# A decoder layer with a mixture of experts on one core: new order in the attention rounds, and the first shared unit made inside their last ones

## The chip, the cores and the metric

The kernel runs on 1 core of one Trainium2 chip. The metric is the device time of one execution in microseconds (us). Before the change it is 1107.71 us, the median of 3 runs (1106.47 to 1108.61).

## The reference, cut to what matters

Three blocks, each followed by a layer norm, on `x` of shape (32, 128, 256) in float32:

```
x = layernorm(x + attention_1(x))        # einsum('nqhd,nkhd->nhqk') on a transposed Q, K: in each token its 16 heads attend to one another
x = layernorm(x + cross_attention(ctx, ctx, x))   # one head of width 256
x = layernorm(x + ffn(x))
def ffn(X):                                   # B x S = 4096 tokens of width 256
    h = rmsnorm(X, norm1_w); q, k, v = h @ wq, h @ wk, h @ wv      # 16 heads of 16
    X = X + softmax(q k^T / 4) v @ wo
    h2 = rmsnorm(X, norm2_w)
    topw, topi = top_k(softmax(h2 @ router_w), 2); topw = softmax(topw)
    shared = (silu(h2 @ sh_gate) * (h2 @ sh_up)) @ sh_down         # 256 -> 512 -> 256
    spec   = sum over the two chosen of 8 experts of topw * (silu(h2 @ e_gate) * (h2 @ e_up)) @ e_down
    return X + shared + spec
```

## The kernel before, in words

All products are made to nearly full float32 precision from two float32r parts: a value is split into `hi` (a copy on ScalarE, ACT) and `lo` (value minus hi, on VectorE, DVE, or GpSimd, POOL), and each product is hi x hi + hi x lo + lo x hi, three matmuls.

**Phase A** (`phase_a`) is the attention part: 16 pairs of batch rows, 256 tokens each. The work on a pair is cut into jobs. Names ending in 1 belong to the first attention (`qk1`, `s1`, `t1`, `o1`, `out1`), names with x to the cross attention (`qx`, `sx`, `pvx`, `vo`), names ending in 3 to the third (`q3`, `k3`, `v3`, 16 heads over 128 tokens, scores `s3`, transposed scores `s3t`, `pv3`, `out3`), and `turn_h2`, `logits`, `turn_lg` make the router's logits. `SCHEDULE` (lines 65 to 86) gives for each engine an ordered list of (job, lag). In iteration `it` an engine runs its list from front to back, each job on pair `it - lag` if that is between 0 and 15. So each engine has one fixed order, written out by hand, and what decides the time is where an engine has to wait for another. The same job can stand at the end of a list with lag L or at its front with lag L+1: the order is the same, only the seam of the list is elsewhere. I write `v1`(15) for job v1 of pair 15.

`BANK` (line 87) gives each TensorE job its PSUM bank. A job waits until the last reader of the bank's previous user is done (`bank_users`, `LAST_READ`); for `o1_0`, `o1_1` that reader is the DVE multiply `o1e_0`, `o1e_1` (line 821), for `s3_0` it is the maximum `max3_0` (line 875), for `pv3_1` the DVE job `e3_1`.

SP (`@block.sync`) issues the DMAs in its own list's order and waits in that order too. `load_q1`, `load_k1`, `load_v1` bring the first attention's operands back from scratch memory; `load_k1` and `load_v1` are eight DMAs each, of 32 KB, into the block diagonals `kbd` and `vbd` (line 338). `s1` needs the first two, `o1` needs `vbd`. `load_kept` (line 349) waits for `qk1_0`, `qk1_1` and `v1` of pair 15, since the shared weights take the room of the first attention's weights, and then issues three weight loads of 512 KB and two token loads of 256 KB. It stands ahead of iteration 19 (`PAIRS + 3`).

**Phase B** (`phase_b`) is the feed-forward part in units of 256 tokens: 8 shared units, then 40 expert tiles (31 full ones and 9 of half size) with gathered rows, then 8 shared units. A unit is, on TensorE, the gate and up products in two halves (`gate_up(n, 0)`, `gate_up(n, 1)`, 24 matmuls each) and the product down (`down_unit`, 24). `gate_up(n + 1, h)` waits until DVE's `product(n, h)` has read the PSUM banks. ACT makes silu (its own table load, as exp has), then `product_hi`; DVE makes `product`, `product_lo`, `tok_lo`. The routing runs on DVE between the halves of the first units, placed by `ROUTING` (line 1783): choose the two experts, count (with two matmuls of TensorE), find slots, spread them as 0/1 matrices (`hits`, `lefts`), which TensorE multiplies in `invert` in units 4 and 5; `read_inverse` then gives the row lists with which POOL gathers rows (`fetch_tile`). `place` gives the table of experts, for which SP waits before it loads the first expert's weights (`load_expert(0)`). POOL makes half of the spread matrices (line 1871) in two instructions.

At the seam between the phases all engines join. Before the change the first tokens and the shared weights are split there, and unit 0's products follow.

At the end POOL adds the experts' results to the sums by accumulating DMAs, one group of `TOTALS` after the other (line 1917), DVE takes moments (`finish`, by `FINISHED`), ACT normalizes (`normalize`, by `NORMALIZED`), SP stores.

## Time and profile before

| | |
|---|---|
| device time, median of 3 | 1107.71 us (1106.47 to 1108.61) |
| the profiled execution | 1107.43 us, its span 1105.6 us |
| mean granted TensorE clock | 0.976 |
| TensorE busy | 1006.2 us, 91% |
| DVE busy | 838.6 us, 76% |
| ACT busy | 675.1 us, 61% |
| POOL busy | 506.3 us, 46% |

The span runs from the first to the last instruction. Phase A ends near 594 us, the shared units run until about 689, the expert tiles until about 1010. Busy shares are means over stages. A row of the timeline has the start, the duration, engine, line, operation, output and inputs, the shape and the number of instructions merged; in brackets stands the idle time of the engine just before and what ended it. A row without a bracket followed the engine's previous instruction at once. "PEclk" is the granted TensorE clock as a share of full speed.

### The profile page before, as it was taken

What the parts mean: (1) busy time and instruction counts of PE and PEld (TensorE: products, weight loads), DVE (VectorE), ACT (ScalarE), POOL (GpSimd) and SP (SyncE); (2) the same over time, 40 slices, a digit from 0 to 9 for tenths busy, and PEclk for the clock granted to TensorE, in tenths of its full rate; (3) what the DMA queues carried; (4) which work ended last, traced back from release to release, by engine and by line L of the source; (5) the groups of instructions that cost most, each with busy time, mean ns of one, the idle gap of its engine ahead of it and who ended that gap; (6) DMA issues with size and microseconds to landing.
All of it is one profiled execution on the core that took longest, in us unless ns stands there. A gap on an engine that the chain in (4) does not pass through costs nothing. (4 is left out here: it accounts for less than half of the span.)

```text
span 1105.6 us, 30332 instructions
## 1 busy us (share of the span) xinstructions
PE 1006.2 (91%) x11710; PEld 939.2 (85%) x11710; DVE 838.6 (76%) x1564; ACT 675.1 (61%) x1435; POOL 506.3 (46%) x525
## 2 busy tenths in 40 slices
PE   5789999999999999998765889999999999999984
PEld 4678888888888888887654889999999999999984
DVE  2767888888888888887665895878888888886445
ACT  2246556667655667666654333777777777775335
POOL 4254454455454455445321022566766556563222
PEclk9999999999999999999986999999999999999998
DMA  7864354544554444441312314689887777761973
GB/s 204 159 104 85 58 106 77 109 101 84 107 107 87 100 104 81 94 88 40 106 36 86 73 34 154 226 247 359 261 277 264 239 271 240 272 239 53 209 172 114
DMA packets 273711, 161.22 MB, mean 146 GB/s; under 512 B 213473, under 2 KB 238945, under 8 KB 272929
## 3 DMA queue, kind: packets, MB, share of 16 engines
q1 hardware_dynamic: 262576, 127.62, 43.0%
q0 software_dynamic: 9408, 29.18, 10.0%
q10 hardware_dynamic: 1584, 2.49, 0.7%
q8 instruction: 94, 1.54, 0.6%
q14 instruction: 49, 0.39, 0.1%
HBM read 120.54 MB, written 38.70 MB: 144 GB/s over the span
## 5 line engine op out<-in xcount | busy, mean ns | idle before, releaser
L1884 POOL DMA_INDIRECT kept_weights<-h_scratch,source_row x71 | 99.1, 1396 | 122.2 <-DVE tok_lo L1733 84.5
L1893 POOL DMA_INDIRECT results_scratch<-kept_late,result_row x71 | 95.0, 1339 | 50.5 <-ACT kept_late L1449 33.3
L1431 ACT ACTIVATE act_hi<-prod 128x512 fp32r<-128x512 f32 x94 | 59.3, 631 | 75.9 <-DVE prod L1744 74.5
L687 ACT ACTIVATE p3t<-psum 128x512 f32<-128x512 f32 x128 | 68.7, 596 | 48.0 <-PE psum L533 48.0
L1744 DVE TENSOR_TENSOR prod<-kept_weights,up 128x512 f32<-128x512 f32 (+1 forms) x112 | 71.6, 640 | 26.1 <-PE up L1315 14.4
L1402 ACT ACTIVATE we_hi<-w_raw 128x1024 fp32r<-128x1024 f32 x81 | 85.7, 1058 | 5.4 <-PE down L1337 5.4
L961 POOL TENSOR_TENSOR ctx_lo<-ctx_t,ctx_hi 128x512 fp32r<-128x512 f32 x16 | 20.5, 1283 | 124.9 <-ACT ctx_hi L597 124.9
L875 DVE TENSOR_REDUCE max<-psum 128x16 f32<-128x2048 f32 x32 | 73.2, 2287 | 5.0 <-PE psum L519 4.7
L1424 ACT ACTIVATE kept_weights<-gate 128x512 f32<-128x512 f32 (+1 forms) x112 | 62.3, 556 | 24.0 <-PE gate L1315 22.8
L1753 DVE TENSOR_TENSOR act_lo<-prod,act_hi 128x512 fp32r<-128x512 f32 x94 | 65.7, 699 | 13.7 <-ACT act_hi L1431 13.4
L378 PE MATMUL psum<-kept_room,x_hi 128*128 128x512 f32 (+1 forms) x256 | 61.5, 363 | 11.9 <-POOL x_lo L957 11.9
L1720 DVE TENSOR_TENSOR we_lo_second<-w_raw,we_hi 128x1024 fp32r<-128x1024 f32 x42 | 51.3, 1221 | 12.0 <-issue 8.1
L378 PEld LDWEIGHTS psum<-kept_room,x_hi 128*128 128x128 f32 x256 | 41.7, 194 | 19.1 <-issue 14.9
L907 DVE RECIPROCAL rden<-rden 128x256 f32<-128x256 f32 x32 | 56.1, 1753 | 1.1
L1720 DVE TENSOR_TENSOR we_lo<-w_raw,we_hi 128x1024 fp32r<-128x1024 f32 x39 | 47.6, 1219 | 8.8 <-ACT we_hi L1402 8.1
L1315 PE MATMUL gate<-tok_hi,we_hi 128*128 128x256 f32 x248 | 51.3, 288 | 0.0
L1449 ACT ACTIVATE kept_late<-down,slot_weights 128x256 f32<-128x256 f32 x71 | 30.1, 470 | 33.1 <-PE down L1337 33.0
L1315 PE MATMUL up<-tok_hi,we_hi 128*128 128x256 f32 x248 | 50.0, 283 | 0.0
L1315 PE MATMUL up<-tok_lo,we_hi 128*128 128x256 f32 x248 | 50.0, 283 | 0.0
L1315 PE MATMUL gate<-tok_lo,we_hi 128*128 128x256 f32 x248 | 49.9, 283 | 0.0
L968 POOL TENSOR_TENSOR x_res<-x_res,b_o 128x512 f32<-128x512 f32 x16 | 21.0, 1313 | 62.2 <-DMA x_res<-in_x 62.2
L1337 PE MATMUL down<-we_hi,act_hi 128*128 128x256 f32 x284 | 48.0, 291 | 0.0
(335 smaller groups left out, 3455.7 us busy)
## 6 DMA issues: line engine op xcount, KB each, us to landing
w_raw<-in_w_gate SPq DMA_DIRECT2D x27, 512.0 KB
w_raw<-in_w_up SPq DMA_DIRECT2D x27, 512.0 KB
w_raw<-in_w_down SPq DMA_DIRECT2D x27, 512.0 KB
raw_gate<-in_w_gate SPq DMA_DIRECT2D x13, 512.0 KB
passed<-in_w_up SPq DMA_DIRECT2D x13, 512.0 KB
passed<-in_w_down SPq DMA_DIRECT2D x13, 512.0 KB
x_t<-in_x_t SPq DMA_DIRECT2D x16, 256.0 KB, 3.4
q_scratch<-qk SPq DMA_DIRECT2D x16, 256.0 KB, 2.4
```

Source lines behind the costliest of these rows:

```text
L378: mm = pe.matmul(dst, x(dk), y(dk), start=(n == 1), stop=(n == 3 * DK))
L687: act.activation(p3t[:, a, 4 * j:4 * j + 4, :], bank[f"s3t_{a}"][:, 512 * j:512 * (j + 1)].rearrange("p (h n) -> p h n", h=4), ACT.Exp)\
L875: half_step(dve.tensor_reduce(max3[:, a, :], bank[f"s3_{a}"].rearrange("p (h n) -> p h n", h=H), AX.X, ALU.max, negate=True))
L1315: mm = pe.matmul(bank[:, fi * UT:(fi + 1) * UT], wp[:, kind, dk * DFF + f * P:dk * DFF + (f + 1) * P], hp[:, n % 2, dk, :], start=(m == 0) ...
L1402: act.activation(w_hi[:, kind, :], raw_of(use)[kind], ACT.Copy).then_inc(w_hi_done, 1)
L1424: act.activation(used(silu[:, h, :], n), used(gate[h][:, :], n), ACT.Silu).then_inc(silu_done, 1)
L1431: act.activation(act_hi[:, n % 2, h * FH:(h + 1) * FH, :], prod[:, h, :].rearrange("p (f n) -> p f n", f=FH), ACT.Copy).then_inc(act_hi_do ...
L1720: dve.tensor_tensor(w_lo[:, kind, :], raw_of(use)[kind], w_hi[:, kind, :].bitcast(F32), ALU.subtract).then_inc(w_lo_done, 1)
L1744: dve.tensor_tensor(used(prod[:, h, :], n), used(silu[:, h, :], n), used(up[h][:, :], n), ALU.mult).then_inc(prod_done, 1)
L1753: dve.tensor_tensor(act_lo[:, n % 2, h * FH:(h + 1) * FH, :], prod[:, h, :].rearrange("p (f n) -> p f n", f=FH), act_hi[:, n % 2, h * FH:( ...
L1884: pool.indirect_dma_start(out=slot_rows[:, i % 2, j, :], out_offset=None, in_=by_token, in_offset=bass.IndirectOffsetOnAxis(ap=source_row[ ...
L1893: pool.indirect_dma_start(out=scratch["results"], out_offset=bass.IndirectOffsetOnAxis(ap=result_row[:, at:at + 1], axis=0), in_=y_rows[:, ...
```

## The change

1. `SCHEDULE` and `BANK` are replaced. Seen as one endless order, the differences are: on TensorE `to1_1` before `turn_h2`; `logits` before `s3t_0`; `s3t_0` before `qk1_0`; `s3t_1` before `qk1_1`; `s1_1`, `pv3_0`, `out3`, `turn_lg` in this order; `v1` behind `pv3_1`; `q3` before `t1_1`; `o1_0` before `vo`. On ACT `norm_h`, `exp1_0` and `h_hi` stand so that `pvc_0` follows `h_hi`; `sq_h2` and `norm_h2` stand behind `x_hi` and `qxe`; `lgc` behind `ctx_hi`. On DVE `den1_0` and `h_lo` stand before `e3_0`, `r3_0` follows `e3_0` at once, `o1e_0` stands before `voe`, `o3_lo` behind `qk1_1e`, `x3` behind `sub1_1`. On POOL `x_lo` is first after `norm_x1`, and `sum` follows `o3e_1`. On SP `load_ctx` goes before `load_res`, `store_h2` stands between `load_k1` and `load_q1`, `store_sum` before `load_v1`.
2. `load_kept` stands ahead of iteration 17 (`PAIRS + 1`). With the new seam of SP's list, iteration 17 begins with `store_sum`(9), `load_v1`(14), `store_q1`(15).
3. The shared weights' hi parts are made on ACT behind `x1_hi`(15), `qxe`(15), `expx`(15), their lo parts on DVE behind `x1_lo`(15), `voe`(15), `bn2`(15); two units' tokens behind `pxe`(15) on ACT and `h_lo`(15) on DVE.
4. Unit 0's gate and up halves are made on TensorE ahead of `turn_h2`(14) and `turn_h2`(15).
5. In phase B unit 0 has only silu, products and down left; the routing starts half a unit to a unit later; POOL's spread is cut into pieces of 4 picks; `TOTALS`, `FINISHED` and `NORMALIZED` are reordered.

```diff
@@ constants
-FINISHED = (0, 0, 0, 2, 4, 8, 10, 14)
-NORMALIZED = (0, 0, 0, 0, 2, 4, 8, 10)
+FINISHED = (0, 0, 0, 2, 4, 8, 12, 14)
+NORMALIZED = (0, 0, 0, 0, 2, 4, 8, 12)
...
+    "pe": [
+        ("t1_0", 2), ("turn_x1", 3), ("q3", 4), ("t1_1", 2), ("k3", 4), ("o1_0", 2), ("vo", 3), ("s3_0", 4),
+        ("qx", 3), ("o1_1", 2), ("to1_0", 2), ("sx", 3), ("tm_0", 4), ("s3_1", 4), ("to1_1", 2), ("turn_h2", 6),
+        ("turn_px", 3), ("v3", 4), ("pvx", 3), ("logits", 6), ("s3t_0", 4), ("qk1_0", 0), ("tm_1", 4), ("out1", 2),
+        ("s3t_1", 4), ("qk1_1", 0), ("s1_0", 1), ("s1_1", 1), ("pv3_0", 4), ("out3", 5), ("turn_lg", 6),
+        ("turn_h", 3), ("pv3_1", 4), ("v1", 0),],
...
+        ("max3_0", 5), ("o1e_1", 3), ("o1lo_0", 3), ("maxx", 4), ("qs_0", 5), ("max3_1", 5), ("recx", 4),
+        ("o1lo_1", 3), ("z2", 4), ("bn2", 4), ("qs_1", 5), ("qk1_0e", 1), ("y1", 3), ("bn1", 3), ("qk1_1e", 1),
+        ("o3_lo", 6), ("max1_0", 2), ("sub1_0", 2), ("max1_1", 2), ("sub1_1", 2), ("x3", 6), ("lge", 7),
+        ("den1_0", 2), ("h_lo", 4), ("e3_0", 5), ("r3_0", 5), ("v1e", 1), ("e3_1", 5), ("x1_lo", 3), ("r3_1", 5),
+        ("den1_1", 2), ("o1e_0", 2), ("voe", 3),],
...
+    "sp": [
+        ("store_sum", 8), ("load_v1", 3), ("store_q1", 2), ("load_x", 1), ("load_ctx", 3), ("load_res", 3),
+        ("store_v1", 2), ("store_h2t", 8), ("load_k1", 2), ("store_h2", 7), ("load_q1", 2),],
...
-    "s3_0": (0, 1, 2, 3), "tm_0": (6,), "s3t_0": (0, 1, 2, 3), "pv3_0": (7,), "s3_1": (0, 1, 2, 3),
+    "s3_0": (0, 1, 2, 3), "tm_0": (4,), "s3t_0": (0, 1, 2, 3), "pv3_0": (4,), "s3_1": (0, 1, 2, 3), "tm_1": (7,),
...
+LAST = PAIRS - 1
+READY = 2
+SPLIT_SHARED = {("x1_hi", LAST): 0, ("qxe", LAST): 1, ("expx", LAST): 2}
+LOWER_SHARED = {("x1_lo", LAST): 0, ("voe", LAST): 1, ("bn2", LAST): 2}
+TOKENS_HIGH = ("pxe", LAST)
+TOKENS_LOW = ("h_lo", LAST)
+UNIT_IN_DRAIN = {("turn_h2", LAST - 1): 0, ("turn_h2", LAST): 1}
@@ phase_a, sync
-                    if it == PAIRS + 3:
+                    if it == PAIRS + 1:
                         load_kept()
@@ phase_a, tensor
+                def first_unit(h):
+                    if h == 0:
+                        pe.wait_ge(kept["tok_lo_done"], READY)
+                        pe.wait_ge(kept["w_lo_done"], len(KINDS))
+                    for b in (2 * h, 2 * h + 1):
+                        job, pair = [(job, pair) for job, pair in in_order("pe") if b in BANK[job]][-1]
+                        after(pe, LAST_READ[job], pair)
...
+                    for mm in half_unit(pe, h, gate, up, kept["tok_hi"][:, 0], kept["tok_lo"][:, 0], kept["ws"][:, 0], kept["ws"][:, 1]):
+                        mm.then_inc(kept["gate_up_ready"], 1)
                 def step(job, pair):
                     prepare(job, pair)
+                    if (job, pair) in UNIT_IN_DRAIN:
+                        first_unit(UNIT_IN_DRAIN[job, pair])
@@ phase_a, scalar, behind step(job, pair)
+                    if (job, pair) in SPLIT_SHARED:
+                        k = SPLIT_SHARED[job, pair]
+                        act.wait_ge(kept["loaded"], 16 * len(KINDS))
+                        for user in ("s1_0", "s1_1", "to1_0", "to1_1"):
+                            after(act, user, LAST)
+                        act.activation(kept["ws"][:, 0, k, :], kept["weights"][:, k, :], ACT.Copy).then_inc(kept["w_hi_done"], 1)
...
@@ phase_b
-        TOTALS = [range(8, 10), range(10, 13), range(13, PAIRS), range(0, 4), range(4, BEFORE)]
+        TOTALS = [range(8, 10), range(10, 13), range(0, 4), range(4, BEFORE), range(13, PAIRS)]
...
-                load_unit(3, 3)
+                for u in range(3, BEFORE):
+                    load_unit(u, u)
                 sp.wait_ge(table_done, 1)
                 load_expert(0)
-                for u in range(4, BEFORE):
-                    load_unit(u, u)
...
                 for n in range(UNITS):
-                    gate_up(n, 0)
+                    if n >= 1:
+                        gate_up(n, 0)
+                    if n == 0:
+                        continue
...
+                    if n == 1:
+                        count_choices()
...
-                token_hi(0)
-                route(None)
-                for kind in range(3):
-                    split(0, kind)
...
+                silu_half(0, 0)
+                silu_half(0, 1)
+                route(None)
+                product_hi(0, 0)
+                product_hi(0, 1)
+                for n in range(1, UNITS):
...
-                ROUTING = {(0, 0): (choose_second,), (0, 1): (weigh, count_tiles), (1, 0): (find_slots,), (1, 1): (find_blocks, place),
-                           (2, 0): (lambda: hit_blocks(0),), (2, 1): (lambda: hit_blocks(1),), (3, 0): (lambda: hit_places(0),),
-                           (3, 1): (lambda: hit_places(1),), (4, 0): (lambda: hit_places(2),), (4, 1): (lambda: hit_places(3),),
-                           (5, 1): (read_inverse,)}
+                ROUTING = {(0, 0): (choose_first,), (0, 1): (choose_second,), (1, 0): (weigh,), (1, 1): (count_tiles,), (2, 0): (find_slots,),
+                           (2, 1): (find_blocks, lambda: hit_blocks(0)), (3, 0): (lambda: hit_blocks(1),),
+                           (3, 1): (lambda: hit_places(0),), (4, 0): (lambda: hit_places(1),), (4, 1): (lambda: hit_places(2),),
+                           (5, 0): (lambda: hit_places(3),), (5, 1): (place, read_inverse)}
                 largest()
-                token_lo(0)
-                for kind in range(3):
-                    split_lo(0, kind)
-                choose_first()
...
-                    picks = slice(half * B, (half + 1) * B)
-                    pool.tensor_tensor(spread[:, picks, SLOTS:2 * SLOTS], hits[:, picks, :],
+                    for at in range(half * B, (half + 1) * B, PIECE):
+                        picks = slice(at, at + PIECE)
...
```

## Rows read from the trace of the kernel before

**Rows 1.** Busy time by stage: stretch, length, PE, PEld, DVE, ACT, POOL; clock, DMA.

```profile
200.00:300.00 100.00, 96.51 (x1483) 85.57 (x1485) 83.69 (x167) 65.26 (x168) 49.40 (x60) 1.00 0.48 97
700.00:800.00 100.00, 100.00 (x841) 100.00 (x840) 81.96 (x132) 76.35 (x129) 64.33 (x48) 1.00 0.84 279
```

**Rows 2.** Who waited for line 821; and PE's timeline of one round.

```profile
  PE psum L525: 15.7, 13
...
280.60 0.44 PE L525 MATMUL psum<-ident,neg_max 128*128 128x128 f32 x2 [1.17 <-DVE p L821]
```

**Rows 3.** DVE's timeline of the same round: `x3`, `max3_0`, `o1e_1`.

```profile
262.52 0.69 DVE L914 TENSOR_TENSOR x<-psum,x 128x512 f32<-128x512 f32 x1 [1.19 <-PE psum L378]
...
277.26 2.28 DVE L875 TENSOR_REDUCE max<-psum 128x16 f32<-128x2048 f32 x1
...
279.86 0.69 DVE L821 TENSOR_TENSOR p<-psum,rden 128x512 f32<-128x512 f32 x1
```

**Rows 4.** SP's DMA queue, 440 to 540: start, total issue time of the merged DMAs.

```profile
447.12 7.62 SPq L338 DMA_DIRECT2D vbd<-v_scratch  x8
...
531.20 0.40 SPq L354 DMA_DIRECT2D kept_weights<-in_w_gate  x1
...
532.60 1.04 SPq L357 DMA_DIRECT2D kept_tokens<-h2t_scratch  x2
```

**Rows 5.** PE's timeline: `pv3_1`(13) and `o1_0`(14).

```profile
463.86 1.08 PE L543 MATMUL psum<-p3t,v 128*32 128x128 f32 x32
...
470.64 1.08 PE L464 MATMUL psum<-vbd,p1t 128*32 128x128 f32 x32
```

**Rows 6.** Line 338 (the block diagonals `kbd`, `vbd`): issue to landing.

```profile
DMA to landing us min/median/max: 2.3/2.9/6.4
```

**Rows 7.** Line 357 (the two token loads of `load_kept`): issue to landing.

```profile
DMA to landing us min/median/max: 7.9/7.9/7.9
```

**Rows 8.** PE's timeline: `turn_h2`(14), unit 0's first matmuls, the count.

```profile
579.11 1.09 PE L399 MATMUL psum<-ident,kept_late 128*128 128x128 f32 x4 [4.43 <-ACT kept_late L651]
...
598.51 0.77 PE L1315 MATMUL gate<-tok_hi,ws_hi 128*128 128x256 f32 x2 [4.24 <-DVE ws_lo L1720]
...
609.74 0.67 PE L1386 MATMUL down<-w_raw,tri 128*128 128x256 f32 x2 [2.69 <-DVE w_raw L1572]
```

**Rows 9.** Timelines of DVE, POOL and ACT during the seam and the routing.

```profile
597.14 3.50 DVE L1720 TENSOR_TENSOR ws_lo<-kept_weights,ws_hi 128x1024 fp32r<-128x1024 f32 x3 [0.83 <-ACT ws_hi L1402]
600.55 0.41 DVE L1561 TENSOR_REDUCE row_sum<-w_raw 128x32 f32<-128x256 f32 x1
...
612.20 0.68 DVE L1585 TENSOR_TENSOR_SCAN w_raw<-w_raw,down 128x256 f32<-128x256 f32 x1
...
624.48 0.69 DVE L1744 TENSOR_TENSOR prod<-kept_weights,up 128x512 f32<-128x512 f32 x1
...
638.29 2.51 DVE L1657 TENSOR_TENSOR hits<-spread_consts,slot_block 128x2272 bf16<-128x2272 f32 x1
...
641.93 3.49 DVE L1726 TENSOR_TENSOR tok_lo<-kept_tokens,tok_hi 128x512 fp32r<-128x512 f32 x1
...
645.94 2.28 DVE L1662 TENSOR_TENSOR lefts<-spread_consts,slot_place 128x2048 bf16<-128x2048 f32 x1
...
640.89 3.98 POOL L1871 TENSOR_TENSOR spread<-hits,spread_consts 128x2272 bf16<-128x2272 bf16 x1 [3.06 <-DVE hits L1657]
...
610.87 1.28 ACT L1424 ACT_TABLE_LOAD   x1
```

**Rows 10.** PE's timeline: the second inversion.

```profile
666.33 2.20 PE L1349 MATMUL turned<-spread,lefts 128*128 128x142 bf16 x32
```

**Rows 11.** Timelines of POOL, DVE and PE near the end.

```profile
1049.05 0.85 POOL L1917 DMA_DIRECT2D acc<-results_scratch  x1 [7.76 <-DMA acc<-results_scratch]
...
1063.54 0.75 DVE L1773 BATCH_NORM_STATS2 stats_b<-acc 128x6 f32<-128x256 f32 x2 [7.86 <-DMA acc<-results_scratch]
...
1068.51 0.80 PE L1315 MATMUL gate<-tok_hi,ws_hi 128*128 128x256 f32 x2 [4.94 <-DVE tok_lo L1726]
```

More of the change, by code:

```diff
@@ L142, with half_unit @@
 SPLIT_LATER = {("den1_1", 0): (3, 4), ("o1e_1", 0): (5, 6)}
+LAST = PAIRS - 1
[5 more added lines that the diff above has]
+UNIT_IN_DRAIN = {("turn_h2", LAST - 1): 0, ("turn_h2", LAST): 1}
+def half_unit(pe, h, gate, up, tok_hi, tok_lo, w_hi, w_lo):
+    for kind, bank in ((0, gate), (1, up)):
+        for fi in range(FH):
+            f = h * FH + fi
+            terms = [(wp, hp, dk) for wp, hp in ((w_hi, tok_hi), (w_hi, tok_lo), (w_lo, tok_hi)) for dk in range(DK)]
+            for m, (wp, hp, dk) in enumerate(terms):
+                mm = pe.matmul(bank[:, fi * UT:(fi + 1) * UT], wp[:, kind, dk * DFF + f * P:dk * DFF + (f + 1) * P],
+                               hp[:, dk, :], start=(m == 0), stop=(m == 3 * DK - 1))
+        yield mm
 def phase_a(nc, t, scratch, sem, kept):
@@ L728, in step_and_weights @@
                     step(job, pair)
+                    if (job, pair) in SPLIT_SHARED:
[4 more added lines that the diff above has]
+                        act.activation(kept["ws"][:, 0, k, :], kept["weights"][:, k, :], ACT.Copy).then_inc(kept["w_hi_done"], 1)
+                    if (job, pair) == TOKENS_HIGH:
+                        for user in ("o1_0", "o1_1"):
+                            after(act, user, LAST)
+                        for u in range(READY):
+                            act.wait_ge(kept["tokens_loaded"][u], 16)
+                            act.activation(kept["tok_hi"][:, u], kept["tokens"][:, u], ACT.Copy).then_inc(kept["tok_hi_done"], 1)
                     if (job, pair) == ("x_hi", 0):
@@ L923, in step_and_weights @@
                     step(job, pair)
+                    if (job, pair) in LOWER_SHARED:
+                        k = LOWER_SHARED[job, pair]
+                        dve.wait_ge(kept["w_hi_done"], k + 1)
+                        dve.tensor_tensor(kept["ws"][:, 1, k, :], kept["weights"][:, k, :], kept["ws"][:, 0, k, :].bitcast(F32),
+                                          ALU.subtract).then_inc(kept["w_lo_done"], 1)
+                    if (job, pair) == TOKENS_LOW:
+                        for u in range(READY):
+                            dve.wait_ge(kept["tok_hi_done"], u + 1)
+                            dve.tensor_tensor(kept["tok_lo"][:, u], kept["tokens"][:, u], kept["tok_hi"][:, u].bitcast(F32),
+                                              ALU.subtract).then_inc(kept["tok_lo_done"], 1)
                     if (job, pair) == EVACUATED_AFTER:
@@ L1115, in phase_b @@
         shift = sb("shift", [P, B])
-        gate = [ctx.enter_context(nc.psum_tensor(f"gate{i}", [P, FH * UT], F32)) for i in range(2)]
-        up = [ctx.enter_context(nc.psum_tensor(f"up{i}", [P, FH * UT], F32)) for i in range(2)]
-        down = [ctx.enter_context(nc.psum_tensor(f"down{i}", [P, 2 * D], F32)) for i in range(2)]
-        turned = [ctx.enter_context(nc.psum_tensor(f"turned{i}", [P, DK * UT], F32)) for i in range(2)]
+        banks = [kept["psum"][:, 512 * b:512 * (b + 1)] for b in range(8)]
+        gate, up, down, turned = banks[0:4:2], banks[1:4:2], banks[4:6], banks[6:8]
         loaded = sem("b_loaded")
```

67 lines of the change are left out of this document (40 added, 27 removed), and 31 rows, old and new, of tables (BANK, SCHEDULE).

## The prediction

> **What bounds it now.** I read the stage table first. In the attention's steady rounds and again in the expert tiles TensorE is busy 96 to 100% at full clock [rows 1]; there only TensorE's own gaps are worth anything. The gaps were then looked up by who ended them. In the attention they are one wait per round: the transposes `tm_0` start after 1.17 us of idling for the DVE multiply `o1e_1`, in 13 rounds 15.7 us together [rows 2]. In the same round DVE comes to the maximum `max3_0` at 277.26 and to `o1e_1` at 279.86 with no idle time ahead of either: DVE is late by its own queue, after it had idled earlier in the round, 1.19 us before `x3` alone [rows 3]. Outside the steady part the losses are the drain of the last pairs, the seam between the phases, the routing during the shared units, and one DMA wait at the end [rows 8 to 11].
>
> **1. New order and banks (steady rounds).** No work is added. `tm_0` moves from bank 6, which `o1_1` holds until `o1e_1` has read it, to bank 4, so it needs `max3_0` alone. `den1_0`, `h_lo` and `r3_0` move into DVE's gaps. I walked one round from `s3_0` at 0 with this trace's durations: TensorE's work adds up to 31.75 us against a round of 32.9. DVE runs without a gap from `x3` at 22.1 to `max3_0` at 33.1, where its scores are ready at 33.0; it ends at 35.7 and `tm_0` is due at 37.0, a slack of 1.3. The next smallest slacks are 0.8 (`v1` behind `x3`) and 1.2 (`turn_h` behind `norm_h`). So the wait of 1.17 goes and nothing replaces it: 12 rounds, 14.0. Ends: 0 (another wait of that size) and the whole 15.7. I take **-14**.
>
> **2. `load_kept` two rounds earlier, on SP's queue.** This is the edit that speaks against the change. It now stands before iteration 17 of SP's list, and its first act is to wait for `v1` of pair 15. Behind it wait `store_sum`(9) and then the eight `vbd` loads of `load_v1`(14), which were issued at 447.12, long before [rows 4]. In the new order `v1`(15) is the matmul group behind `pv3_1`, so it ends where that one did, at 464.9; `o1_0`(14) needs the `vbd` blocks and stood at 470.64, less 1.5 for `vo`, which now follows it: 469.2 [rows 5]. TensorE reaches it 4.3 us after `v1`(15). SP in that time: waking 0.2, five DMAs of `load_kept` 2.5 (531.20 to 533.64), `store_sum` 0.5, eight `vbd` issues 7.6 [rows 4], landing 2.9 [rows 6]: 13.7, a stall of 9.4. Low end: landing 2.3 and issues as fast as the other DMAs here, 0.5 each: 13.7 - 3.6 - 0.6 - 4.3 = 5.2. High end: the 2 MB of weights and tokens occupy the DMA engines until 9.8 us after the first issue (tokens issued at 533.1, landed 7.9 later [rows 4, 7]), and the blocks only then: 0.2 + 9.8 + 7.6 + 2.9 - 4.3 = 16.2. TensorE then restarts slowly: after the 4.24 of idle time at the seam a unit's 48 matmuls took 609.74 - 2.69 - 598.51 = 8.5 us [rows 8], against 48 x 0.119 = 5.7 in the tiles (841 in 100 us) [rows 1]. That is 2.8, of which I take 2.6. TensorE has no slack in this round, so all of it arrives at the end: **+12** (7 to 19).
> The Trainium skill ("DMA: Bandwidth & Descriptors", section "Two DMAs through the same engine are not ordered") says that descriptors of one queue start in order on each DMA engine. The trace shows no small load behind a large one. By the rule the stall would be the high end, 16 rather than 9, and the total about 7 us worse.
>
> **3. The drain.** Three ACT splits of 1.0 us (as DVE's of the same tile), three DVE ones of 1.17 (3.50 for three [rows 9]) and two pairs of token splits (0.6 each) leave the seam and enter rounds in which DVE and ACT partly bound TensorE. Laid over the timeline of the last two rounds (estimates), the two DVE splits ahead of `max3_0`(14) delay `tm_0` by about 1.6, the one after `bn2`(15) delays `qs_1`(14) and so `s3t_1` by 0.7; on ACT 0.3 is left before `k3` is evacuated: +2.6. The gate and up halves of unit 0 (24 matmuls each, 2.9 us warm) go into the gaps before `turn_h2`(14) and (15); the first was 4.43 us long [rows 8], the second 0.6 shorter. They cost nothing if warm, 2 if the second runs at half clock (5.7); if the gaps closed they would cost their 5.8. They also keep the clock up for `out3`(15), worth about 1. `h_hi` before `pvc_0` brings `h_lo` forward 0.8 in two rounds; `o3e_1` before `sum` and `r3_0` before `e3_1` bring `out3`(15) forward by 1.2 (POOL is in `sum` when the reciprocal ends). Net **-1.5** (-4 to +4).
>
> **4. Seam and shared units.** Before: from the attention's last TensorE work (598.51 - 4.24 = 594.27) to the second inversion at 666.33 it takes 72.1 us [rows 8, 10]. TensorE's largest gaps there are the seam's 4.24 and 2.69 for the count. After: unit 0 is ready at the seam, and DVE becomes the bound, since routing and products share it. DVE's chain: silu's table load 1.28 [rows 9], silu 0.6: first product at 596.8. Its own work for units 0 to 5, up to the last `lefts`: 31 operations of 0.6 = 18.6. Five handshakes of 0.7 with ACT, 3.5. New waits: 2.0 (`product_lo`(0,0) is queued on ACT behind the exp and its table load), 1.5 (`weigh` waits for the ratio, which ACT takes after silu(1,1) and another table load). Routing: both choices 600.55 to 612.20 less 4.6 of unit work = 7.1; `weigh` 0.6; count and `find_slots` 612.20 to 624.48 less 2.0 = 10.3; `find_blocks` 0.9; two `hits` of 2.45 and four `lefts` of 2.25 = 13.9 [rows 9]. Sum 655.2. POOL's spread was one instruction of 3.98 us, and DVE's `tok_lo` that began within it took 3.49 instead of 0.68 [rows 9]; cut into eight pieces it delays DVE's two-input operations by up to one piece (0.5) each: +1.5, 656.7. TensorE, let go by the `lefts` before, runs the first inversion until 649.1 and then unit 5's halves (2 x 2.9) and unit 4's down product (2.9), to 657.8; the second inversion starts there, 8.5 earlier than 666.33. Of this I keep 7, as TensorE's restarts after DVE waits (one of 5 us behind `find_slots`) may not all be hidden. Behind the inversion TensorE's work is the same; `place` moved behind it in time, so expert 0 is fetched at 661 and due at 670, and the rows' gather keeps its distance to `turn`(8). Cover there is some 3 us; if it is gone, that much comes back. Ends: -2 (the DVE waits after choices double) and -10. **-7**.
>
> **5. The end.** DVE waits 7.86 us, until 1063.54, for the results of pairs 0 to 3, and TensorE idles 4.94 for the tokens behind it, then restarts slowly; its idle time had been preceded by full load, so of the 2.8 above I take 1.6 [rows 11]. In the new `TOTALS` their group is third, not fourth. One step of that queue is 1049.05 back to the issue before its wait of 7.76, 7.8 us: it lands at about 1055.8, and DVE comes to it at 1055.7. Pairs 13 to 15 go last and are due near 1080. That frees 6.5; the moments moved a unit earlier free 0.5. **-7** (-4 to -8).
>
> **Sum.** The profiled execution took 1107.4 (span 1105.6 and 1.8 around it), 0.3 below the median of the runs. 1107.4 - 14 + 12 - 1.5 - 7 - 7 = **1090**.
>
> **Rivals.** (a) *No stall at `load_v1`*: the loads are still early enough. For it speaks only that the other seven DMAs before `vbd` are quick; against it the queue's order, which leaves 4.3 us for 13.7 of issue. 1107.4 - 29.5 = 1078. (b) *The order gives nothing*: DVE's gapless chain of 13.6 us slips by its 1.3 of slack and the 1.17 stays, 1104. For it: so long a chain without a gap; against: the bank wait goes in any case. (c) *DVE's chain is too long, slower than before*: `tm_0` waits for `max3_0` itself, in 12 rounds. With a wait of w the time is 1107.4 - 3.5 (points 2 to 5) + 12 (w - 1.17); it passes the time before at w = 1.46, that is when DVE comes 2.8 later than I walked it, and at w = 2.6 it is 1121. For it: `h_hi` now stands ahead of `pvc_0` on ACT and waits for `turn_h`, in every round; against: with that I still found 1.3 to spare. (d) *A long stall*, 20 instead of 12 in point 2: 1098. (e) *The edits do not meet the seam*: TensorE still idles there for silu and products as long as for the splits now, and point 4 gives 2: 1095.
>
> **Chances.** Forecast with its neighbours (d) and (e), 0.66; (a) 0.15; (b) 0.10; (c) 0.09. About 0.2% (2.2 us) is what a measurement can tell from no change. Range for 8 in 10: 1076 (a, a little better) to 1103 (b and long stalls); the likeliest case's own is 1082 to 1099. Faster 0.87, same 0.04, slower 0.09.
>
> **What would show it.** `tm_0` without a wait and a round of 31.8 us (point 1). A TensorE gap of 5 to 16 us ended by the `vbd` DMA ahead of `o1_0`(14), with eight `vbd` issues behind five large ones (point 2). Unit 0's matmuls in both `turn_h2` gaps (point 3). DVE almost gapless from the seam to the inversion, which starts about 63 us after the attention's end (point 4). No DMA wait of DVE near the end (point 5). A round still of 32.9, or no `vbd` wait, would show 1 or 2 wrong.

## The result and the profile after

The changed kernel takes **1100.76 us** (median of 3 runs, 1100.74 to 1101.36) against 1107.71: a ratio of 0.994 (95% interval 0.9917 to 0.9963), 7 us faster. The forecast was 1090 with a range of 1076 to 1103: right in sign and inside the range, but less than half of the 17 us came. One execution of a kernel below (e10) took 1953.84 us where its other five took 1078 to 1084; it is left out of that kernel's figure, and its cause is not known.

The spans fell from 1105.6 to 1098.9, by 6.7. Four marks of TensorE's timeline tell where: the attention's last transpose `turn_lg`(15), the second inversion, the turn of the first tile's tokens (`turn`(8)) and the last turn of a tile.

| Stretch | before | after | difference | forecast |
|---|---|---|---|---|
| start to the attention's end | 594.3 | 594.9 | +0.7 | -3.5 |
| of it: order, from a run below | | | -13.7 | -14 |
| of it: stall at `load_v1`, from a run below | | | +9.5 | +12 |
| of it: the drain, what is left | | | +4.9 | -1.5 |
| to the second inversion (seam, routing) | 72.1 | 68.5 | -3.5 | -7 |
| to `turn`(8) | 19.4 | 19.3 | -0.1 | 0 |
| the tiles, to the last turn | 318.0 | 313.6 | -4.4 | 0 |
| the end | 101.9 | 102.5 | +0.6 | -7 |

The stage table of the changed kernel (stretch, length, PE, PEld, DVE, ACT, POOL with counts; clock, DMA) answers to [rows 1]:

```profile
200.00:300.00 100.00, 100.00 (x1512) 88.87 (x1510) 88.51 (x172) 69.08 (x173) 50.52 (x60) 1.00 0.49 102
...
455.00:465.00 10.00, 2.80 (x24) 2.59 (x23) 5.30 (x9) 4.54 (x11) 3.73 (x6) 0.81 0.87 253
465.00:475.00 10.00, 8.70 (x121) 7.67 (x122) 3.93 (x5) 0.99 (x3) 2.50 (x2) 0.68 0.80 188
...
700.00:800.00 100.00, 100.00 (x852) 99.86 (x851) 83.43 (x136) 77.11 (x130) 65.12 (x50) 1.00 0.85 285
```

In the attention's steady rounds TensorE now has no gap at all: 1512 matmuls in 100 us for 1483, and a round of 31.84 us (from `s3_0` to `s3_0`, 237.49 to 269.33) for 32.91 (241.24 to 274.15). In the tiles it does 852 for 841 and was busy 100% both times: there is no gap that could have been closed, so the matmuls themselves are quicker. Between them lie 10 us in which it is busy for 2.8.

That hole is the stall. PE's and SP's timelines (start, duration, what; in brackets the idle time before and who ended it) answer to [rows 4, 5]:

```profile
453.72 0.35 SPq L378 DMA_DIRECT2D kept_weights<-in_w_gate  x1
...
455.07 1.10 SPq L381 DMA_DIRECT2D kept_tokens<-h2t_scratch  x2
456.21 0.44 SPq L365 DMA_DIRECT2D sum_scratch<-kept_late  x1
456.81 6.97 SPq L362 DMA_DIRECT2D vbd<-v_scratch  x8
...
466.30 1.94 PE L502 MATMUL psum<-vbd,p1t 128*32 128x128 f32 x32 [8.51 <-DMA vbd<-v_scratch]
```

It waited 8.51 us (forecast 9.4), and `o1_0`(14) then ran 1.94 us for 1.08, while the granted clock was 0.50 of full speed (1.2 of 2.4 GHz) from 463 to 469 and 0.68 in the mean of the second 10 us above. TensorE had been idle since 457.8.

The DMA view of 453 to 467 gives the size of the loads and the median from issue to landing:

```profile
kept_tokens<-h2t_scratch SPq DMA_DIRECT2D x2, 256.0 KB, 6.0
vbd<-v_scratch SPq DMA_DIRECT2D x8, 32.0 KB, 4.7
```

The blocks' packets, 64 bytes each, start at 461.3 only, 4.5 us behind their first issue, when the weights have landed and the tokens nearly; all large transfers are done by about 462.5, before the last block is issued. So the large loads delay the first blocks but not the last.

The round of pair 14, whose steps stand on three engines (DVE first, then ACT, then PE):

```profile
528.43 0.63 DVE L893 TENSOR_TENSOR vo<-psum,b_vo 128x512 f32<-128x512 f32 x1
531.36 1.23 DVE L977 TENSOR_TENSOR ws<-kept_weights,ws 128x1024 fp32r<-128x1024 f32 x1 [2.30 <-ACT ws L772]
532.50 2.29 DVE L925 TENSOR_REDUCE max<-psum 128x16 f32<-128x2048 f32 x1
...
529.54 0.84 ACT L658 ACTIVATE qx_t<-psum,b_qx 128x256 f32<-128x256 f32 x2 [2.17 <-PE psum L402]
530.27 1.05 ACT L772 ACTIVATE ws<-kept_weights 128x1024 fp32r<-128x1024 f32 x1
...
535.33 0.66 PE L563 MATMUL psum<-ident,neg_max 128*128 128x128 f32 x2 [3.72 <-DVE neg_max L931]
535.91 2.09 PE L557 MATMUL psum<-k,q 32*128 32x128 f32 x32
...
545.87 1.60 PE L571 MATMUL psum<-qs,k 32*128 32x128 f32 x32 [2.15 <-ACT p3t L725]
```

DVE is free at 529.1 and reaches its second lower split of the shared weights. The high half of it is made by ACT, behind `qxe`(15), which itself waits for TensorE; so DVE stands idle for 2.30 us with `max3_0`(14) queued behind, whose scores were ready at 527.9. TensorE waits 3.72, and the next scores take 2.09 instead of 1.17.

The seam (timelines of ACT and PE) answers to [rows 8 to 10]:

```profile
623.62 0.63 ACT L1472 ACTIVATE tok_hi<-kept_tokens 128x512 fp32r<-128x512 f32 x1 [6.51 <-DMA kept_tokens<-h2t_scratch]
...
598.17 0.77 PE L1370 MATMUL psum<-tok_hi,ws 128*128 128x256 f32 x2 [3.23 <-DVE prod L1807]
...
625.03 0.80 PE L1370 MATMUL psum<-tok_hi,ws 128*128 128x256 f32 x2 [3.26 <-DVE tok_lo L1789]
...
653.80 1.19 PE L1404 MATMUL psum<-spread,lefts 128*128 128x142 bf16 x16 [3.38 <-DVE lefts L1725]
...
663.48 2.20 PE L1404 MATMUL psum<-spread,lefts 128*128 128x142 bf16 x32
```

TensorE still idles where unit 0's products are due; later ACT waits 6.51 for unit 3's tokens, and TensorE 3.26 behind it, and 3.38 in the first inversion for DVE's second `lefts`. POOL's pieces, by groups (count, total busy, mean ns, idle before):

```profile
L1932 POOL TENSOR_TENSOR spread<-hits,spread_consts 128x284 bf16<-128x284 bf16 x16 | 18.5, 1195 | 41.2 <-DVE hits L1720 41.2
```

And the end (POOL, ACT, DVE, PE), to [rows 11]:

```profile
1052.34 0.85 POOL L1979 DMA_DIRECT2D acc<-results_scratch  x1 [8.71 <-DMA acc<-results_scratch]
...
1055.20 2.08 ACT L1520 ACTIVATE acc<-acc,shift,rstd_b 128x256 f32<-128x256 f32 x4 [8.47 <-POOL shift L1998]
...
1057.79 0.69 DVE L1807 TENSOR_TENSOR prod<-kept_weights,psum 128x512 f32<-128x512 f32 x1 [7.87 <-ACT kept_weights L1486]
...
1060.93 0.80 PE L1370 MATMUL psum<-tok_hi,ws 128*128 128x256 f32 x2 [5.02 <-DVE tok_lo L1789]
```

DVE's wait for the DMA is gone, and in its place it waits 7.87 for ACT, which waits 8.47 for POOL's `shift`, which POOL makes only behind its last add, at 1052.34, which waits 8.71 for a DMA. TensorE waits 5.02 us where it waited 4.94. In the kernel before, ACT's same operation had waited too, and ended its wait 2.2 us before DVE's:

```profile
1061.32 2.08 ACT L1458 ACTIVATE acc<-acc,shift,rstd_b 128x256 f32<-128x256 f32 x4 [6.96 <-POOL shift L1936]
```

The chain of waits (start, length, what; from its seven longest pieces) agrees: its longest is this DMA, and the late tokens are on it too.

```profile
614.59 8.95 DMA kept_tokens<-h2t_scratch
...
1020.36 12.81 DMA acc<-results_scratch
1034.00 18.05 DMA acc<-results_scratch
```

### The profile page after: what moved, and what is told of

The parts are those of the page before. It is cut to its first block and busy times, and to the rows that moved or that the text cites. A ratio compares the mean times of both kernels' runs of the same rounds, so it can differ in the third digit from the quotient of the medians.

```text
span 1098.9 us, 30360 instructions
## 1 busy us (share of the span) xinstructions
PE 1008.3 (92%) x11710; PEld 941.5 (86%) x11710; DVE 845.5 (77%) x1564; ACT 682.6 (62%) x1437; POOL 521.0 (47%) x539
## 5 line engine op out<-in xcount | busy, mean ns | idle before, releaser
L1370 PE MATMUL psum<-tok_hi,ws 128*128 128x256 f32 x480 | 86.6, 299 | 17.5 <-DVE prod L1807 9.3
L1370 PE MATMUL psum<-tok_hi,we_hi 128*128 128x256 f32 x496 | 100.7, 284 | 0.0
L1370 PE MATMUL psum<-tok_lo,we_hi 128*128 128x256 f32 x496 | 99.0, 281 | 0.0
L1807 DVE TENSOR_TENSOR prod<-kept_weights,psum 128x512 f32<-128x512 f32 (+1 forms) x112 | 71.7, 641 | 32.5 <-ACT kept_weights L1486 16.6
L1370 PEld LDWEIGHTS psum<-tok_hi,ws 128*128 128x128 f32 x480 | 72.8, 206 | 18.8 <-DVE tok_lo L1789 8.7
L1017 POOL TENSOR_TENSOR x_lo<-x_t,x_hi 128x512 fp32r<-128x512 f32 x16 | 20.5, 1279 | 142.6 <-ACT x_hi L631 142.5
L1370 PEld LDWEIGHTS psum<-tok_lo,we_hi 128*128 128x128 f32 x496 | 76.1, 189 | 0.0
L1370 PEld LDWEIGHTS psum<-tok_hi,we_hi 128*128 128x128 f32 x496 | 75.9, 189 | 0.1
L1486 ACT ACTIVATE kept_weights<-psum 128x512 f32<-128x512 f32 (+1 forms) x112 | 62.2, 557 | 20.0 <-PE psum L1370 19.7
L1370 PE MATMUL psum<-tok_hi,we_lo 128*128 128x256 f32 x320 | 63.7, 280 | 0.0
```

The lines of the kernel that those rows point to most:

```text
L1370: mm = pe.matmul(bank[:, fi * UT:(fi + 1) * UT], wp[:, kind, dk * DFF + f * P:dk * DFF + (f + 1) * P], hp[:, n % 2, dk, :], start=(m == 0) ...
L1486: act.activation(used(silu[:, h, :], n), used(gate[h][:, :], n), ACT.Silu).then_inc(silu_done, 1)
L1807: dve.tensor_tensor(used(prod[:, h, :], n), used(silu[:, h, :], n), used(up[h][:, :], n), ALU.mult).then_inc(prod_done, 1)
```

## The experiments

Ratios are to the kernel before, in runs on the same chip (its medians were 1108.0 to 1109.1).

| Kernel | us | ratio (95%) | attention's end | to second inversion | tiles |
|---|---|---|---|---|---|
| after | 1100.76 | 0.994 (0.9917 to 0.9963) | 594.9 | 68.5 | 313.6 |
| e1 order alone | 1094.68 | 0.9876 (0.9855 to 0.9896) | 580.5 | 72.2 | 318.9 |
| e2 | 1091.60 | 0.9846 (0.9822 to 0.9870) | 585.4 | 69.4 | 314.3 |
| e3 | 1093.33 | 0.9861 (0.9841 to 0.9881) | 595.2 | 69.4 | 313.6 |
| e4 pad 32 | 1097.30 | 0.9888 (0.9870 to 0.9907) | 594.4 | 69.3 | 311.1 |
| e5 | 1099.59 | 0.9928 (0.9915 to 0.9941) | 591.6 | 69.6 | 315.4 |
| e6 | 1099.35 | 0.9926 (0.9913 to 0.9939) | 595.4 | 67.3 | 314.2 |
| e7 | 1102.85 | 0.9944 (0.9931 to 0.9957) | 596.3 | 70.9 | 314.7 |
| e8 pad 480 | 1104.99 | 0.9973 (0.9962 to 0.9985) | 594.7 | 69.1 | 318.5 |
| e9 pads 96, 32 | 1103.34 | 0.9952 (0.9936 to 0.9968) | 594.0 | 69.3 | 315.8 |
| e10 five edits | 1080.93 | 0.9741 (0.9724 to 0.9757) | 585.4 | 68.2 | 314.2 |
| e11 with pads | 1076.71 | 0.9701 (0.9686 to 0.9717) | 584.7 | 66.8 | 310.6 |
| e12 before, pad 64 | 1102.39 | 0.9931 (0.9915 to 0.9947) | 594.2 | 73.0 | 313.1 |
| e13 | 1079.06 | 0.9731 (0.9713 to 0.9749) | 581.9 | 68.4 | 313.6 |
| e14 with pads | 1075.66 | 0.9703 (0.9684 to 0.9722) | 583.3 | 68.3 | 310.4 |

The marks come from one profiled execution each and have a spread of their own: e3, e4, e8 and e9 have the changed kernel's attention and seam untouched and gave 594.0 to 595.2 and 69.1 to 69.4, against its 594.9 and 68.5. The ratio of the changed kernel itself has the widest interval, about 2.5 us to either side: what differs from it by less (e5, e6, e7) is not clear in the time and rests on the marks.

**e1, the order alone.** The kernel before with the two tables of the changed one and nothing else:

```diff
-SCHEDULE, BANK = (before)
+SCHEDULE, BANK = (after)
```

> The kernel before with the new job order and banks alone. Theory (the order is worth what the forecast said, and the drain's loss comes from the split and lower jobs put into it): 1107.7 - 14 = 1094, no TensorE wait in the steady rounds, and the pair of rounds at the end of the attention no longer than before. Rival (the new order itself lengthens the drain, in which fewer jobs fill each round): 1098 to 1100, the round from s3_0(14) to s3_0(15) near 32 us as in the changed kernel. On the tiles: there TensorE took a 128x256 matmul every 119.3 ns before and every 117.5 in the changed kernel; if this comes from where the operands lie in SBUF, it is 119.3 here; if from anything in the order, 117.5.

Measured 1094.68, 13.4 below: the forecast's -14 stands, and the rival (the order lengthens the drain) falls: `s3_0`(14) to `s3_0`(15) took 25.8 us here, 26.1 before and 32.4 in the changed kernel. The tiles were as slow as before, so the order is not what quickened them:

```profile
700.00:1000.00 300.00, 299.59 (x2512) 299.18 (x2511) 245.12 (x394) 227.96 (x386) 181.34 (x135) 1.00 0.75 252
```

The other edits together, then, made the kernel 6 us slower.

**e2, `load_kept` behind `load_v1`(14).**

```diff
-                    if it == PAIRS + 1:
-                        load_kept()
                     for job, lag in SCHEDULE["sp"]:
...
+                            if (job, it - lag) == ("load_v1", LAST - 1):
+                                load_kept()
```

> The changed kernel with load_kept behind load_v1(14) on SP's queue. Theory: the whole stall of 8.51 us ahead of o1_0(14) and the slow restart behind it (about 1) go and stay gone: 1100.8 - 9.5 = 1091. Rival 1 (given back in the drain, since the weights land 8 us later relative to the work and the splits wait): 1096 or more. Rival 2 (store_q1(15) and load_k1(15) are now late behind load_kept's five DMAs): a wait for kbd in its place, 1097 to 1101.

1091.60: 9.2 less, and all of it stays. The eight `vbd` issues now stand 16 us ahead of `load_kept`, take 4.08 us instead of 6.97, and `o1_0`(14) starts with no wait and at full speed; both rivals fall.

```profile
437.25 4.08 SPq L363 DMA_DIRECT2D vbd<-v_scratch  x8
453.12 0.36 SPq L379 DMA_DIRECT2D kept_weights<-in_w_gate  x1
...
457.13 1.08 PE L503 MATMUL psum<-vbd,p1t 128*32 128x128 f32 x32
```

Against this kernel `o1_0`(14) is 9.2 us later in the changed one (466.30 for 457.13) and `o1_1`(14) 11.4 (473.90 for 462.49): the stall and 2.2 for the slow restart. By the attention's end 9.5 is left. The attention ends at 585.4 here and at 580.5 in e1: 4.9 us (within about 1) are the price of the drain.

**e3, `root(0)` ahead of the last add** (`root(k)` are POOL's four small operations that give `shift`).

```diff
                 for g in range(len(TOTALS)):
+                    if g == len(TOTALS) - 1:
+                        root(0)
                     add_results(1, g)
...
-                for k in range(PAIRS // 2):
+                for k in range(1, PAIRS // 2):
                     root(k)
```

> The changed kernel with POOL's root(0) ahead of the last add of results instead of behind it. Theory: ACT waits 8.47 us in normalize for root(0), which stands behind an add that waits 8.71 us for its DMA; with root(0) ahead this goes, TensorE's wait of 5.02 and its slow restart too: 1100.8 - 7 = 1094. Rival 1 (the next wait takes its place: root(1) still stands behind the last add, or DVE's moments wait for the results of pairs 0 to 3, group 3 of the queue): 1098 to 1100. Rival 2 (the end is set by the last normalizes in any case): 1100.

1093.33: 7.4 less. ACT's first normalize starts without a wait and the second waits 0.82; TensorE's gap of 5.02 is gone. From the tiles' last turn to the end it now takes 93.6 us for 102.5, and 101.9 before: the wait for POOL was all that kept the end from its gain.

```profile
1047.54 0.21 POOL L1993 TENSOR_TENSOR shift<-neg_mean,rstd_b 128x4 f32<-128x4 f32 x1
1053.58 0.94 POOL L1979 DMA_DIRECT2D acc<-results_scratch  x1 [5.83 <-DMA acc<-results_scratch]
...
1047.78 2.08 ACT L1520 ACTIVATE acc<-acc,shift,rstd_b 128x256 f32<-128x256 f32 x4
...
1057.25 2.08 ACT L1520 ACTIVATE acc<-acc,shift,rstd_b 128x256 f32<-128x256 f32 x4 [0.82 <-POOL shift L1993]
```

**e4, e8, e9, e12: where the operands lie.** In SBUF, tok, act_hi, act_lo and all weights of the second phase started at 3744 modulo 4096 in the kernel before. The change moved the first two and the shared weights to 128 and left the others. (These addresses are worked out from the order and sizes of the allocations; no trace shows them. Each padding moves everything allocated behind it too.)

```diff
         WC = DK * DFF
+        pad = sb("pad", [P, 8])      # e4; 120 in e8; 24 in e9, with 8 more ahead of act_lo
```

```diff
# e12, in the kernel before
+        pad = sb("pad", [P, 16])
         tok_hi = sb("tok_hi", [P, 2, DK, UT], F32R)
```

> The changed kernel with 32 bytes of padding in front of the second phase's own SBUF tensors: the experts' weights then start at a multiple of 64 bytes, as tok_hi and act_hi do already, instead of at 32 over one. Theory 'alignment' (operands at 32 over a multiple of 64 cost TensorE reads): the tiles' matmuls go from 117.5 ns to 116 or less, -4 to -8 us: 1093 to 1097. Theory 'same residue' (moving and stationary operand collide when their addresses agree modulo some power of two; before they all agreed modulo 4096, now only act_lo and the weights do): no change, 117.5 ns, or slower where the residues now agree modulo 64. Null: the cadence has nothing to do with addresses, 1100.8.

> As the kernel with 32 bytes of padding, with 480: the second phase's own tensors then start at 128 modulo 4096, where tok_hi and act_hi start too, and are multiples of 64 as with 32. Theory 'alignment' (32 bytes gave 115.4 ns a matmul for 117.5, at a residue of 3776): 115.4 again, 1097. Theory 'residue' (operands whose addresses agree modulo 4096 collide): 117.5 or slower, 1101 or more.

> The changed kernel with 96 bytes in front of the second phase's tensors and 32 in front of act_lo. Addresses modulo 4096: tok and act_hi 128, weights 3840, act_lo 3872; so weights less tok is 128 modulo 256 and 0 modulo 128, act_lo less weights is 32. So far a difference of 0 modulo 4096 gave 120.0 ns between matmuls, 32 modulo 128 gave 118.5 (tok with weights), 64 modulo 128 gave 114.4. Theory 'period 128 or shorter': the matmuls of tok with weights go back to 120 ns, those of act_lo with weights fall from 119 to 118 or less; about 1102 us. Rival 'longer period': tok with weights stays at 114 to 117 and the time at 1095 to 1097.

> The kernel before with nothing but 64 bytes of padding in front of tok_hi: tok, act_hi and act_lo then lie 64 bytes from the weights modulo 4096, where all had the same residue. Theory (where the operands lie, and nothing else of the change, made the tiles' matmuls faster): 119.3 ns falls to about 115, the tiles' 318 us to about 309: 1107.7 - 8 = 1100. Rival (DVE bounds the tiles once TensorE is faster): 1103 to 1105. Null: 1107.7.

The same stretch of e4, e8 and e12, in this order, after the rows of before and of the changed kernel:

```profile
700.00:1000.00 300.00, 300.00 (x2519) 300.00 (x2518) 248.06 (x399) 230.30 (x390) 185.12 (x136) 1.00 0.77 260
```
```profile
700.00:1000.00 300.00, 300.00 (x2555) 299.86 (x2554) 252.35 (x406) 233.17 (x394) 185.55 (x137) 1.00 0.77 259
```
```profile
700.00:1000.00 300.00, 298.49 (x2573) 297.60 (x2573) 252.50 (x407) 236.29 (x399) 187.28 (x139) 1.00 0.77 259
```
```profile
700.00:1000.00 300.00, 299.79 (x2515) 299.58 (x2514) 247.91 (x398) 229.88 (x389) 185.91 (x137) 1.00 0.77 259
```
```profile
700.00:1000.00 300.00, 298.64 (x2558) 297.72 (x2557) 251.49 (x403) 235.12 (x396) 180.11 (x137) 1.00 0.78 261
```

From start to start a gate or up matmul took 120.0 ns before and 118.2 after (the 119.3 and 117.5 of the expectations are means over all matmuls of one line, transposes too); with 32 bytes of padding 114.9, with 480, where all residues modulo 4096 agree again, 119.9. In the kernel before, 64 bytes alone gave 117.0 and 1102.39: 6.7 less than the unpadded kernel in the same runs (1109.13). So the places of the tensors in SBUF set part of a matmul's time: shown by taking the gain away (e8) and by making it in the old kernel (e12). That it is the two operands of TensorE which matter, and not the other tensors that a padding moves along, is the reading of these runs and not shown. Alignment to 64 bytes is not it (e8 has it too). A period of 128 bytes isn't either: e9 came to 118.9 for both pairs of operands, neither 120 nor 114. The rule stays open. The padded e12 also shows the rival's part: waits for DVE's `tok_lo` (1.4 us) appear in the tiles, and the tiles took 313.1 instead of the expected 309.

**e5, the lower splits out of the way.**

```diff
-LOWER_SHARED = {("x1_lo", LAST): 0, ("voe", LAST): 1, ("bn2", LAST): 2}
+LOWER_SHARED = {("x1_lo", LAST): 0, ("qs_1", LAST - 1): 1, ("o3_lo", LAST - 2): 2}
```

> The changed kernel with DVE's second and third lower split of the shared weights moved behind qs_1(14) and o3_lo(13), out of the way of max3_0(14) and qs_1(14). Theory (DVE idles 2.30 us at LOWER 1 for ACT's split, which is queued behind qxe(15), and max3_0(14), tm_0 and the scores stand behind it; TensorE then runs at half clock): the wait of 3.7 us before tm_0(14) and what follows it go, the round from s3_0(14) to s3_0(15) falls from 32.4 to about 28, the attention ends 4 to 5 earlier: 1096. Rival (the round is long because of ACT, whose splits delay exp3 of pair 14, seen as waits of s3t on exp3_03): the round stays above 31, 1099 to 1101.

```profile
527.84 0.63 DVE L893 TENSOR_TENSOR vo<-psum,b_vo 128x512 f32<-128x512 f32 x1
528.39 2.28 DVE L925 TENSOR_REDUCE max<-psum 128x16 f32<-128x2048 f32 x1
...
532.32 0.41 PE L563 MATMUL psum<-ident,neg_max 128*128 128x128 f32 x2 [1.30 <-DVE neg_max L931]
```

`max3_0`(14) follows `vo` at once, the wait before `tm_0` is 1.30, the round takes 29.0 for 32.4, and the attention ends 3.3 earlier: the mechanism is as said. But the time is 1.2 lower only, which the intervals can't tell from no change. The tiles took 1.8 longer; TensorE waits three times in them for DVE's `tok_lo`, 1.0 us together, and the rest is open.

**e6, unit 3's tokens first.**

```diff
                 load_unit(2, 2)
+                load_unit(3, 3)
                 sp.wait_ge(weighed, 1)
...
-                for u in range(3, BEFORE):
+                for u in range(4, BEFORE):
```

> The changed kernel with the load of unit 3's tokens ahead of SP's wait for the routing weights. Theory (tok_hi of unit 3 waits 6.51 us for that load, DVE 2.8 and TensorE 3.26 behind it): these go, the stretch from the attention's end to the second inversion falls from 68.5 to about 66, 1098.5. Rival (DVE's chain is the bound and was only waiting earlier for what it now waits for later): 68 or more, 1100.8.

`tok_hi` of unit 3 ran at 617.49, 6 us sooner, TensorE's wait there fell from 3.26 to 1.24, but the next one for a product rose from 2.46 to 3.91. The stretch took 67.3, not 66, which is 1.2 less than in the changed kernel's own profile and 1.8 to 2.1 less than in its four siblings; the time is 1.4 lower, inside the noise. The wait goes as the theory says, its worth is somewhat smaller.

**e7, one piece.**

```diff
-PIECE = 4
+PIECE = 32
```

> The changed kernel with POOL's spread in one instruction for each half, as before, not eight. Theory (sixteen pieces took 18.55 us where two took 8, and DVE's two-input operations beside them ran 0.1 to 0.5 us longer each): POOL's part ends earlier, DVE's single operation beside it runs long once or twice (3.5 for 0.7, as before): 2.5 us less in all, 1098.5. Rival (cutting is right: the long collisions of DVE with a POOL instruction of 4 us cost as much as the pieces): 1100 to 1102.

```profile
637.21 3.98 POOL L1932 TENSOR_TENSOR spread<-hits,spread_consts 128x2272 bf16<-128x2272 bf16 x1 [40.10 <-DVE hits L1720]
...
638.18 3.57 DVE L1789 TENSOR_TENSOR tok_lo<-kept_tokens,tok_hi 128x512 fp32r<-128x512 f32 x1
```

1102.85, not 1098.5, and 1.5 to 2.4 longer to the inversion: my theory falls. Against the changed kernel the 2.1 more are inside the noise; against e5 and e6, measured in the same runs, it is 3.3 and 3.5. Sixteen pieces occupy POOL for 18.5 us instead of 8, yet DVE's `tok_lo` takes 0.86 beside them and not 3.57. Added up, DVE's two-input operations ran 3.6 us longer beside the sixteen pieces than alone, and 5.5 beside the two whole instructions (`tok_lo` 3.57, `act_lo` 3.32, each 0.69 alone). The Trainium skill ("SBUF — State Buffer", section "SBUF: two separate sides") says that of a GpSimd operation and a DVE operation with two SBUF inputs, the one that starts first holds their shared ports for the whole instruction; the row agrees (POOL had 3.0 left of its 3.98 when DVE began, and DVE alone takes 0.69). Cutting makes the loss smaller and does not take it away.

**e10, e13: the edits together.** The edits of e2, e3, e5 and e6, and:

```diff
-TOKENS_HIGH = ("pxe", LAST)
+TOKENS_HIGH = ("exp3_13", LAST - 1)      # e10; ("exp3_03", LAST - 1) in e13
```

> The changed kernel with the five edits of order together: load_kept behind load_v1(14), root(0) ahead of the last add, the load of unit 3 ahead of the wait for the weights, two lower splits behind qs_1(14) and o3_lo(13), and the token splits on ACT behind exp3_13(14) instead of pxe(15). Theory (the losses add up, as they lie in different stages): 1100.8 - 9.2 - 7.4 - 1.4 - 1.2 = 1081.5, and the attention ends 13 us earlier than in the changed kernel, near 581. Rival (one wait takes over from another in the seam or the tiles, which start 12 us earlier relative to nothing but their own loads): 1085 to 1088.

> The kernel with all five edits of order, but with ACT's two token splits (1.16 us) behind exp3_03(14), in front of exp3_10(14), where ACT idles 1.29 us, instead of behind exp3_13(14), ahead of norm_h(15). Theory (their place cost the 2.56 us before turn_h(15) and the slow transposes behind it): the round from s3_0(14) to s3_0(15) falls from 31.9 to about 29, the attention ends near 582, 1081.5 - 3 = 1078.5. Rival (anything on ACT in this round is late for norm_h, wherever it stands): 31 or more, 1080 to 1082.

e10 gave 1080.93, close to the 1081.5 expected, but not by the expected stages: its attention ended at 585.4, not 581: ACT's token splits (first fence, from e10) now stood right ahead of `norm_h`, and TensorE waited for it. In e13 (second) they fill a gap: the round takes 29.6 for 31.9, the attention ends at 581.9, and the kernel takes 1079.06, where 1078.5 was expected. The intervals of e10 and e13 overlap, so this step too rests on the marks.

```profile
539.21 1.14 ACT L779 ACTIVATE tok_hi<-kept_tokens 128x512 fp32r<-128x512 f32 x2
540.25 0.90 ACT L690 ACTIVATE h_in<-x,rstd_h 128x256 f32<-128x256 f32 x2
...
541.29 1.09 PE L424 MATMUL psum<-ident,h_in 128*128 128x128 f32 x4 [2.56 <-ACT h_in L690]
```
```profile
529.99 1.17 ACT L779 ACTIVATE tok_hi<-kept_tokens 128x512 fp32r<-128x512 f32 x2
...
537.40 0.63 PE L424 MATMUL psum<-ident,h_in 128*128 128x128 f32 x4 [1.79 <-ACT h_in L690]
```

**e11, e14: with paddings.** e10 with 64 bytes ahead of tok_hi, 32 ahead of the second phase's tensors and 64 ahead of act_lo; e13 with 32 and 64, and tok_hi left where it was.

> The kernel with all five edits of order, and paddings: 64 bytes in front of tok_hi, 32 in front of the second phase's tensors, 64 in front of act_lo. Then each pair of operands that TensorE reads together lies 64 bytes apart modulo 128, the shared weights and their tokens too. Theory: the matmuls of the tiles at 115 ns or less, 1081 - 3.5 = 1077 or better. Rival (DVE is now the bound in the tiles, at 84% busy: the matmuls get faster but waits for it appear): the kernel without paddings less 2 or less.

> The same, with 32 bytes of padding in front of the second phase's tensors and 64 in front of act_lo; tok_hi stays at 128 modulo 4096 (weights 3776, act_lo 3840). Theory (the time of a matmul hangs on where both operands lie, not on their difference alone): tok with weights 114.4 ns again, act_lo with weights about 116 instead of 119.9, 115 in the mean, and 1078.5 - 5 = 1073.5. Rival (116 as in the kernel with the tokens moved, or DVE as the bound): 1075 to 1077.

1076.71 and 1075.66, intervals that overlap: both 3% below the kernel before and faster than both kernels of this case. e11 took the time expected, but its gate and up matmuls 116.6 ns and not 115. e14's theory falls: with tok and the weights at e4's very addresses, the gate and up matmuls took 117.2 ns, not 114.9, once act_lo and what lies behind it had moved (down with act_lo: 116.0 for 119.7). What one pair of operands costs also hangs on something beside its own two addresses.

## Why the prediction was right and wrong

1. **Order and banks: right.** -13.7 at the attention's end, for -14; `tm_0` waits no more in the steady rounds, these take 31.84 us for the 31.75 added up, and rivals (b) and (c) fell.
2. **`load_kept`: right, a little too dear.** The stall was 8.51 for 9.4, and the slow restart behind it 2.2 for 2.6; later rounds gave 1.2 of it back, so 9.5 in all for 12. Rival (a), no stall, and (d), a long one, fell. The prediction's high end of 16 was worked out wrongly: it lets the large loads end and then adds the eight issues, though SP issues while the loads run. The Trainium skill ("DMA: Bandwidth & Descriptors", section "Two DMAs through the same engine are not ordered") says that descriptors of one queue start in order. This trace agrees, since the blocks' packets start at 461.3, behind the weights', but the order costs the stall nothing here: the large transfers were done by about 462.5, the last `vbd` issue ended at 463.8 and `o1_0` ran at 466.3, so a landing of 2.5 behind it, within what [rows 6] have without large loads ahead.
3. **The drain: wrong, +4.9 for -1.5.** The step that failed is "the two DVE splits ahead of `max3_0`(14) delay `tm_0` by about 1.6". From `s3_0`(14) to `tm_0`(14) it took 8.6 us (526.72 to 535.33), and 5.0 in e1 (517.58 to 522.54): a delay of 3.6. The step counted the durations of what was put in and not what it waits for: the second split waits for ACT's, which waits behind `qxe`(15). e5 gave 3.3 of the 4.9 back, and e13 ends its attention 1.4 behind e1. Unit 0's halves have little part in it: from `out3`(15) to `turn_h2`(15) it took 7.1 us (585.00 to 592.06) for 6.7 before (583.86 to 590.58), with the second half in the gap. What the last 1.4 are is open.
4. **The seam: the mechanism right, the size half: -3.5 for -7.** DVE is the bound, as said, but its last `lefts` ended 67.9 us after the attention's end (662.84 less 594.94), and the sum had 62.4 (656.7 less 594.3). Of these 5.5, 2.8 are a wait of DVE for unit 3's tokens: the edit put `load_unit(3)` behind SP's wait for `weighed`, and point 4 has no term for it. Another 2.1 are POOL's pieces: the term for them is 1.5, and DVE's two-input operations ran 3.6 longer beside them in all (two whole instructions cost more, e7). The remaining 0.6 is not traced. Through the wait of 3.38 in the first inversion this reaches TensorE, which began unit 5 5.0 us later than the sum has it. e6 shows that without the token wait 1.2 to 2.1 come back, not 2.8. Rival (e), in which point 4 gives 2, was nearer to what was measured than the forecast.
5. **The end: wrong, +0.6 for -7.** DVE came to the results of pairs 0 to 3 and found them there, as said. The step that failed is "That frees 6.5": only the wait that ended last, DVE's for the DMA, was followed. The second one, ACT's normalize for POOL's `shift`, stood behind the last add in POOL's queue, and had been hidden under the first, ending at 1061.32 where DVE's ended at 1063.54. e3 shows that with POOL's order mended the 7 are there (93.6 us for 101.9).
6. **Not seen at all: -4.4 in the tiles.** The buffers' new places made the matmuls quicker. The prediction wrote that behind the inversion "TensorE's work is the same". With the residues made equal again (e8) the change is worth 0.9973 (0.9962 to 0.9985), 3 us. So more than half of the 7 us measured come from a cause that the prediction does not have. Without it the time is 1105 (e8), outside the range: that the result fell inside was luck.

Steps 3 and 5 are one mistake: a moved operation was priced by its duration and by the wait it ends, not by the chain of its own inputs through other engines' queues.
